# Units of 128 places in the edge list of a graph attention kernel, in place of 256

## What is computed

```python
h = (x_flat @ W_gat).reshape(M, HEADS, NUM_EXPERTS)      # 4 heads x 4 values
e = leaky_relu(a_src[src] + a_dst[dst], 0.2)
ee = exp(e - segment_max(e, dst)[dst])
alpha = ee / (segment_sum(ee, dst)[dst] + 1e-16)
agg = segment_sum(h[src] * alpha, dst) + b_gat           # M x 16
scores = layernorm(agg).reshape(M, HEADS, NUM_EXPERTS).mean(1)
w, i = top_k(scores, 2); w = softmax(w)
out = sum_e gate_e * (gelu(x @ W1[e] + b1[e]) @ W2[e] + b2[e])
```

## Time and profile before

| | |
|---|---|
| median of 3 runs | 4511.31 us (4510.68 to 4512.57) |
| the profiled execution, its own time | 4502.82 us |
| span of the profiled execution | 4501.1 us |
| PE busy | 3514.0 us (78%) |
| DVE busy | 2830.1 us (63%) |
| POOL busy | 2904.8 us (65%) |
| ACT busy | 1131.1 us (25%) |
| mean granted TensorE clock | 0.796 |

### The profile page before, as it was taken

How to read it: one execution, slowest core, us unless ns; L and a number is a source line. 1 busy time by engine, 2 the same in 40 slices (tenths; PEclk the granted TensorE clock), 3 DMA queues, 4 the chain that set the end, 5 groups by cost and what they waited for, 6 DMA issues and landing times. The chain is left out here.

```text
span 4501.1 us, 61920 instructions
## 1 busy us (share of the span) xinstructions
PE 3514.0 (78%) x19005; PEld 2450.4 (54%) x19041; DVE 2830.1 (63%) x3531; ACT 1131.1 (25%) x2825; POOL 2904.8 (65%) x2928
## 2 busy tenths in 40 slices
PE   4686332588837999999999999999999999963143
PEld 1454232455525666666666666666666666663011
DVE  7778999888854454554554544545545545445788
ACT  0110000011103333334334333334343343320000
POOL 3000888787735777777777777777777777774055
PEclk8898555688866888989889888889898888876555
DMA  1243111599982222222222222222222222255099
GB/s 50 58 101 82 52 42 52 52 122 116 120 110 66 33 37 33 36 37 33 36 33 37 36 33 36 37 32 37 36 34 36 36 34 36 34 16 6 17 366 332
DMA packets 307960, 284.72 MB, mean 63 GB/s; under 512 B 203555, under 2 KB 280099, under 8 KB 307365
## 3 DMA queue, kind: packets, MB, share of 16 engines
q1 hardware_dynamic: 209556, 202.96, 20.8%
q0 software_dynamic: 87936, 29.35, 9.8%
q10 hardware_dynamic: 10384, 51.39, 5.3%
HBM read 161.21 MB, written 122.27 MB: 63 GB/s over the span
## 5 line engine op out<-in xcount | busy, mean ns | idle before, releaser
L1097 POOL DMA_INDIRECT gath<-tab_d,src_no x2192 | 2068.4, 944 | 752.7 <-issue 667.7
L463 POOL DMA_INDIRECT edge_d<-run_slots,slots x544 | 672.7, 1237 | 579.0 <-ACT run_slots L662 415.7
L1234 PEld LDWEIGHTS C<-spread,lo_hot 128*128 128x128 f32 x4384 | 804.7, 242 | 312.6 <-issue 215.9
L1234 PE MATMUL C<-spread,lo_hot 128*128 128x160 f32 x4384 | 875.9, 367 | 122.7 <-DVE spread L1394 119.5
L1406 DVE TENSOR_TENSOR acc<-acc,C 128x160 f32 x1096 | 351.7, 321 | 914.3 <-PE C L1234 773.1
L1220 PEld LDWEIGHTS C<-dst_rows,lo_hot_t 128*128 128x128 f32 x4384 | 558.6, 207 | 92.1 <-issue 78.3
L1220 PE MATMUL C<-dst_rows,lo_hot_t 128*128 128x32 f32 x4384 | 575.8, 288 | 12.2 <-ACT lo_hot_t L1115 12.2
L1129 ACT ACTIVATE mlp<-A,b2s 64x392 f32<-64x392 f32 x512 | 298.2, 582 | 943.7 <-PE A L1253 943.7
L1243 PE MATMUL A<-T,w1s 64*128 64x392 f32 x1024 | 530.3, 601 | 0.0
L575 PE MATMUL C<-wide_rec,hot_lo 128*128 128x136 f16 x2048 | 272.1, 305 | 299.1 <-DVE wide_rec L840 299.1
L1253 PE MATMUL A<-hid,w2s 128*64 128x392 f32 x1024 | 452.5, 524 | 0.0
(11 more groups left out here) (268 smaller groups left out, 3266.4 us busy)
## 6 DMA issues: line engine op xcount, KB each, us to landing
mlp_d<-mlp ACTq DMA_DIRECT2D x128, 392.0 KB
mlp<-mlp_d SPq DMA_DIRECT2D x64, 784.0 KB, 6.0
gath<-tab_d,src_no POOLq DMA_INDIRECT x2192
pixels<-in_x SPq DMA_DIRECT2D x32, 392.0 KB, 8.5
src<-in_x SPq DMA_DIRECT2D x32, 392.0 KB, 9.3
T<-t_d SPq DMA_DIRECT2D x128, 98.0 KB
X<-x_d SPq DMA_DIRECT2D x64, 196.0 KB, 7.9
out<-X SPq DMA_DIRECT2D x128, 98.0 KB, 6.6
```

The lines of the kernel that those rows point to most:

```text
L463: pool.indirect_dma_start(edge_d, bass.IndirectOffsetOnAxis(ap=slots[:, k, c:c + 1], axis=0), run_slots[:, k, c * RUN:(c + 1) * RUN, :].re ...
L1097: pool.indirect_dma_start(gath[:, g % BUFS, j, :], None, tab_d, bass.IndirectOffsetOnAxis(ap=src_no[:, t:t + 1], axis=0)).then_inc(gathere ...
L1234: mm = pe.matmul(C[:, bank, at:at + HI * VALS], lo_hot[:, k % UNROLL, u * U + j, :], spread[:, u * U + j].rearrange("p h v -> p (h v)"), s ...
```

## The change

U goes from 2 to 1: a unit is 128 places, 32 runs, one tile, and each quarter of the lanes takes one of a run's four places. UG goes from 8 to 16, so a group is still 16 tiles. MAX_UNITS is now 2132 smaller units, which is NG = 134 groups (TILES = 2144) in place of 137. The loop over groups without MLP disappears, since MLP_TRIPS = TRIPS = 32 and LAST = 6. `raw` needs 17152 words a lane and lies with `lo_hot` in a common tile `arena`. The pads are written in 16 DMAs of 32 rows in place of 8 of 64.

```diff
-U = 2
-UNIT_RUN_BITS = 6
+U = 1
+UNIT_RUN_BITS = 5
 RUN_ROWS = U * P // RUN
 PARTS_U = P // RUN_ROWS
-UG = 8
+UG = 16
 PAIRS = UG // 2
...
-                n = PLACES * RUN * FIELDS // 8
-                for k in range(8):
+                n = PLACES * RUN * FIELDS // 16
+                for k in range(16):
...
-                pool.wait_ge(s["pads_written"], 8 * 16)
+                pool.wait_ge(s["pads_written"], 16 * 16)
...
-            lo_hot = tb("lo_hot", [P, UNROLL, G, P])
+            arena = tb("arena", [P, max(UNROLL * G * P, PLACES * RUN * FIELDS // 2)])
+            lo_hot = arena[:, 0:UNROLL * G * P].rearrange("p (b t l) -> p b t l", b=UNROLL, t=G)
...
-            assert MLP_TRIPS <= TRIPS and UG % 4 == 0 and LAST >= 3
-            raw = lo_hot[:].rearrange("p b t l -> p (b t l)").bitcast(F16)[:, 0:PLACES * RUN * FIELDS]
+            assert MLP_TRIPS == TRIPS and UG % 4 == 0 and LAST >= 3
+            raw = arena[:].bitcast(F16)[:, 0:PLACES * RUN * FIELDS]
...
-                with pe.Fori(MLP_TRIPS, TRIPS) as i:
-                    for k in range(UNROLL):
-                        body(i, k, False)
...
-                row_i = lo_hot[:].rearrange("p b t l -> p (b t l)").bitcast(I32)[:, RAW_WORDS:RAW_WORDS + TILES]
+                row_i = acc[:].rearrange("p q v -> p (q v)").bitcast(I32)[:, 0:TILES]
```

More of the change, by code:

```diff
@@ L1058, in build @@
             LAST = NG - TRIPS * UNROLL
-            assert MLP_TRIPS <= TRIPS and UG % 4 == 0 and LAST >= 3
-            raw = lo_hot[:].rearrange("p b t l -> p (b t l)").bitcast(F16)[:, 0:PLACES * RUN * FIELDS]
-            RAW_WORDS = PLACES * RUN * FIELDS // 2
+            assert MLP_TRIPS == TRIPS and UG % 4 == 0 and LAST >= 3
+            raw = arena[:].bitcast(F16)[:, 0:PLACES * RUN * FIELDS]
             @block.sync
@@ L1179, in _ @@
                         body(i, k, True)
-                with act.Fori(MLP_TRIPS, TRIPS) as i:
-                    for k in range(UNROLL):
-                        body(i, k, False)
                 for k in range(LAST):
@@ L1442, in _ @@
                 dve.tensor_tensor(dev, dev, na[:, :, 1:2].broadcast_to([P, NQ, FEAT]), ALU.subtract).then_inc(s["squares_ready"], 1)
-                scaled = lo_hot[:].rearrange("p b t l -> p (b t l)")[:, 0:NQ * FEAT].rearrange("p (q f) -> p q f", q=NQ)
+                scaled = arena[:, 0:NQ * FEAT].rearrange("p (q f) -> p q f", q=NQ)
                 dve.wait_ge(s["squares_ready"], 1)
```

## The result

The changed kernel takes **5028.17 us** (median of 4 runs, 5014.27 to 5049.07); the kernel before took 4511.0 us in the same batch of runs (4 runs). The ratio is 1.1147, 95% interval 1.1118 to 1.1176: **slower by 11.5%**. Forecast were 4788 us and a range of 4570 to 4980, so the sign and the loop were right and the size was too small. The profiled execution took 5014.27 us, with a span of 5012.4 and a mean granted clock of 0.776 (before: 4502.82, 4501.1, 0.796).

What follows compares the result with a forecast made beforehand. POOL's gathers bound the kernel at 19.96 us a group; the new PE and DVE loop of 20.96 + 0.3 load + 1.4 clock = 22.66 us over 128 groups, with start and end, gave +285 us: 4788 us, range 4570 to 4980.

Steps and rivals of the forecast that it cites:

- POOL loses the bound to a loop of PE and DVE: Group loop with MLP: POOL's 19.96 us a group gives way to a PE and DVE loop of 22.66 us.
- the PE wait in the first half: Middle of PE's first scatter half: PE sits about 1.9 us until DVE has added that half's first pair.
- The sum of 20.96 us at full clock: PE and DVE loop of one group with MLP, before load and clock costs: 20.96 us, over POOL's 19.96.
- seven steps: Parts of the group loop: 0.89, 4.13, 0.23, 0.99, 7.75, 2.02 with 0.61, and 4.34 us.
- rival D: Group loop: DVE loses the gaps between pairs, clock costs nothing, POOL stays the bound; 4454 us, chance 0.06.
- I cost [the load] between nothing and 0.6, I take 0.3: DVE's load of 16 block numbers in place of eight, each group: 0.3 us more taken.
- I take the level to hold to about 19.5, 0.4 + 1.0 = 1.4 us: After PE restarts in the first half, the lower clock holds some 4 us, adding 1.4 us a group.
- rival B: Same loop, lower clock over before the first half ends: period 21.26 us, about 4605 us, chance 0.18.
- rival C: Clock stays low through the whole stretch between the halves: 25.5 us a group, about 5150 us, chance 0.10.
- The mean clock: PE's mean granted clock in the loop falls from 0.88 to about 0.75.
- Start of phase two: Before the first weighing: reading the list for four lane parts adds 10.2 us; four casts of 1.3 us stay hidden.
- Groups without MLP: Five steps behind the 128 groups with MLP: 18.7 us each, 94 us in all.

Runs made afterwards that it cites:

- either edit alone: Kernel before with each add doubled into an unread spare tile, 4502.94 us; or with a wait for each unit, eight waits a group, 4507.47 us.
- reordered: Changed kernel with DVE's pick_damp, load of block numbers and adds of the first two pairs moved ahead of one_hots: 5036.69 us, ratio 1.1198.

## Why the prediction was right, and where it failed

- **POOL loses the bound to a loop of PE and DVE**: right. The weighing no longer waits for gathers, POOL waits for `rows_used` once in each group, and the PE wait in the first half, forecast at 1.9 us, is there, ended by DVE's increment: 1.52 us on the mean of the 128 groups, 2.0 to 2.7 in 75, and under 0.3 in 32, nearly all of them groups in which the lower clock has held PE up before.
- **The sum of 20.96 us at full clock**: right as a floor; no group is under 21.99. Six of the seven steps of the shorter group are within 0.12 us of it. The gap of 0.33 us between pairs stayed also where results waited ([0.33 <-DVE acc] above), so rival D had nothing to stand on. It was 0.25 in the groups without the MLP. The Trainium skill (VectorE: DVE Perf Modes, The DRAIN you can't avoid) says that a semaphore after each operation costs nothing extra; this trace does not bear that out for these adds. The two adds of a pair, with no semaphore between them, follow each other with a gap of 0.785 - 2 x 0.321 = 0.14 us; between pairs, with an increment and a wait as instructions of their own, it is 0.33. No run took the semaphores away, so the 0.19 more is read and not tested.
- **"I cost [the load] between nothing and 0.6, I take 0.3"**: it is 1.100 us for 16 numbers against 0.598 for eight, so 0.50, near the upper end. Spread to first add grew by 1.40 in the shorter group: 0.50 is the load, 0.47 a wait for pick_dst (at the lower clock by then) ahead of pick_damp, and 0.34 more time between pick_damp's end and the first add. That 0.34 stands in the third group of every trip of four; the first has 0.47 more ahead of one_hots. Before there was neither.
- **"I take the level to hold to about 19.5, 0.4 + 1.0 = 1.4 us"**: this step failed. By the means, 24.47 - 20.96 - 0.50 for the load - 0.2 for the two delays above leave 2.8 us a group where I had 1.4 (an estimate from these rows). I took one length for the low stretch, from the earlier trace rows, and let it start before PE restarts, as it does there. In the loop there are two courses. In 74 of 128 groups the low clock is over by the end of the first half or at most some 2 us behind it, near to rival B. In 51 it fills all or most of the stretch between the halves, and in 37 of these it starts only after the wait and runs on into the second half, as in rival C and beyond it: the longer group pays 3.76 us between the halves, 0.75 in the first half and 0.69 behind the start of the second, together 5.2, where C had 3.9. The mean of the two is what the loop costs. I had priced both ends, and given C 0.10, as if every group had to go one way. What decides the course of a group, and why the clock falls only after the restart in the longer ones, stays open; that filling the wait does away with the long stretches is shown.
- **The size of the miss** is this period: (24.47 - 22.66) x 128 = 232 us, where the profiled execution is 226 us over the forecast. Filling the wait takes back 161 us of them; the mis-sized load is 0.2 us a group, 26 us; the two delays that come once in four groups are (0.47 + 0.34) x 32 = 26 us, an estimate; some 19 us were not separated.
- **The mean clock**: forecast 0.75 in the loop, measured 0.81 to 0.85. So I forecast too low an average and still too small a loss. Before, 5.01 us a group at the low clock hid behind POOL; now the low clock stands on the path. Where it falls counts for more than its share.
- **Start of phase two**: 10.2 us forecast, 12.4 measured at the first weighing. The four casts a table of a quarter take 2.07 us each and not 1.3, the decoding grew by 11 us, and of the 13.65 us of wait for `nodes` 2.64 are left: still hidden, but nearly through its cover.
- **Groups without MLP**: 18.2 us a group (4541.70 to 4632.83 for five), forecast 18.7. The last group 13.7, forecast 13.8. ACT's further copies cost nothing, as forecast: in the loop PE waits for no copy of dst_rows.

## What to carry to other kernels

Cutting an accumulation into smaller pieces through the same two PSUM banks makes PE wait for the adds of the very piece of work it is in. Count which adds each matmul waits for, and when the adding engine comes to them; if that is later, try to space the pieces among other work of PE rather than issue them back to back (shown here only where PE itself was slow). A wait of 2 us in a loop of 22 cost another 1.3 us in clock here, and a group that can take either course of the clock is to be priced as a mixture. A kernel whose time has not moved can still have lost its slack: the run with the waits alone had a loop over POOL's, and only the weighings' distance showed it. Before reordering an engine's work, look at what the moved-up operation itself waits for: pick_damp waited 2.13 us.

## What had not been expected of the hardware

- A load of register numbers on DVE costs by the number: 0.598 us for eight, 1.100 for sixteen.
- A low stretch of the clock in the loop was 6.8 us long or shorter in the kernel before, with the wait filled, and with either edit alone; with PE's wait of 2 us inside the half, 40 of 127 (change) and 29 of 127 (reordered) were 13.7 us long. That holds for the batches of the first sort; where PE halts by itself, such stretches stand in other kernels too.
- The body of the loop grew by the adds, and the instruction queue q14 fetched 200 packets in place of 43 (1.64 MB in place of 0.34). DVE has two new delays in each trip of four groups, 0.47 us ahead of hi_hot in the first and 0.34 ahead of the first add in the third, some 26 us in all. That the fetching causes them was not tested.
- A cast that reads a quarter of the lanes takes 2.07 us for 32x2144, where a half took 1.31 for 64x2192: fewer lanes, more time. The source differs as well: it now reads one place of every four in place of two.
- One kernel, unchanged, took 4500 us in some batches and 6440 to 6480 in others, with PE's work halting for 3 to 16 us. The worth of a variant changed between them: the filled wait beats the reordered kernel by 4% in one sort and not at all in the other, and the waits alone cost 0.2% or 7%.
